# Attention's output kept transposed and undivided in DRAM, and divided in one last stage over four batches

## The chip, the cores and the metric

The kernel runs on one core of a Trainium2 chip. The metric is the device time of one execution in microseconds (us).

## The reference

The input `x` has 4 batches of 2048 tokens with 256 features. A first layer (a recurrence gated by a small expert network) and a second layer follow one another. The second layer, cut to what matters here:

```python
xn = _layernorm(x)
q, k, v = (xn @ W.T + b for each), reshaped to 16 heads of 16
a1 = softmax(q1 @ k1.T / 4); x1 = a1 @ v1     # heads 0 to 7
a2 = softmax(q2 @ k2.T / 4); x2 = a2 @ v2     # heads 8 to 15
s = concatenate([x1 - lv * x2, x2]) @ Wp.T + bp
g = silu(mixture_of_experts(xn))
return x + s * g
```

`lv` is one number worked out from four small vectors. Batches times heads make 64 attentions of 2048 queries by 2048 keys.

## The kernel before

The program runs in stages, each a block in which the five engines have instruction lists of their own and meet through semaphores. The first layer and the second layer's experts take the first 2640 us and are not touched. Then `attend` does the 64 heads, and `output_batch` does the projection and the last sum, once for each batch.

**`attend`.** A step is half a head: 1024 queries against all 2048 keys. There are 128 steps (`t`), two for each head (`half`), and each has eight slots (`sl`). In a slot TensorE's list is: three score products (`score`, keys by queries, 128x512), then the extra jobs of some slots, then two peak pairs (`peak`: the scores of the next step the other way round, 128 queries x 1024 keys), a fourth score product, and `values`: eight fp32 products of exponentials with values into O. O lies in bank 7 as 4 groups of 32 partitions by 256 queries; in each group 16 rows are features, and row 16 is the sum of the exponentials, since the values have a column of ones. ScalarE takes the exponential of each score tile (`at_E<-at_ps`), 32 a step. VectorE reduces every peak pair to its maxima (`at_mpart`), and at the end of a step these to `at_mx`.

Peak pairs and extra jobs use a ring of two pairs of banks: TensorE fills one when VectorE has freed it. There are two extra jobs. `turn` in slot 1 transposes `at_mx`; VectorE negates it (`at_mneg`), rounds it to bf16 (`at_mrow`), and takes the remainder as a second, low row; SP moves the two rows into `at_qs`, where the next step's scores subtract them. `normalise` in slot 3 brings the last step's O to queries by features: ScalarE's `copy_out` in slot 1 has put O into `at_osb`, TensorE transposes it in two products, VectorE inverts the eight sums of each query (`at_rec`) and multiplies into `at_A`, which holds all heads in SBUF. `values` of slot 1 starts the next O and waits for `copy_out`.

SP's list: sixteen loads for the head after the next, the values, and the rows of the two steps. GpSimd meanwhile joins the experts' results (`combine_experts`).

**`output_batch`.** For one batch: SP loads `f` (the experts' result) and `x1` (the residual), 2 MB each. VectorE combines the heads of `at_A` into `at_mix` (64 small operations over four batches for `x1 - lv * x2`, 64 copies), TensorE transposes them (32 products a batch), ScalarE copies them into `at_outT`, TensorE multiplies with `wp` (line 1586), VectorE adds the bias (line 1555) and multiplies with silu(f) (line 1558), GpSimd forms the silu and adds the residual (line 1570), and SP stores. A batch ends with a barrier.

## Time and profile before

| | |
|---|---|
| time, median of 3 runs | 5811.28 us (5802.47 to 5816.74) |
| the profiled execution | 5814.46 us, span 5813.0 us |
| granted TensorE clock, mean | 0.961 |
| busy share: TensorE, VectorE, ScalarE, GpSimd | 87%, 74%, 59%, 24% |

The span is from the first to the last instruction; the time of the execution is 1.5 us more. The profiled execution is 3.2 us slower than the median. Busy TensorE time is modelled, since its products are pipelined.

### The profile page before, as it was taken

The page shows a single profiled execution, that of the slowest core. Times are in us where ns is not written, and L with a number is a line of the kernel's source. Part 1 is how long each engine was busy: PE and PEld are TensorE (multiplying, and loading weights), DVE is VectorE, ACT ScalarE, POOL GpSimd, SP SyncE. Part 2 cuts the span into 40 slices and gives each one's busy share as a digit, 9 for nine tenths or more (in the row PEclk, how much of TensorE's full clock was granted, in tenths as well). Part 3 has the DMA queues.
Part 4 walks back from the last instruction along what each step waited for, and adds up shares of the span by engine and source line. Part 5 has one row for each costly group of instructions (what it writes and reads, how often), then busy time and mean ns, then how long its engine had stood idle before and what let it go on. Part 6 is the DMA issues. An engine that isn't in the chain of part 4 may idle for free. (4 is left out here: it accounts for less than half of the span.)

```text
span 5813.0 us, 94556 instructions
## 1 busy us (share of the span) xinstructions
PE 5028.4 (87%) x32123; PEld 2145.5 (37%) x32123; DVE 4317.1 (74%) x5419; ACT 3426.4 (59%) x5923; POOL 1419.5 (24%) x885
## 2 busy tenths in 40 slices
PE   5777777777767999996999999999999999999995
PEld 3233233233234566652333333333333333333334
DVE  5997987987971111115888888888888888888884
ACT  5765765666631111112767777777777777777772
POOL 1855846846850000004750000000000000000005
PEclk8998998998998999997999999999999999999998
DMA  3303003002022211213331111111111111111114
GB/s 100 106 15 116 0 28 104 1 30 87 1 78 83 72 61 62 65 61 86 101 87 32 34 30 29 29 29 34 32 29 29 29 32 34 29 29 29 29 39 163
DMA packets 351454, 299.33 MB, mean 51 GB/s; under 512 B 169184, under 2 KB 320992, under 8 KB 350432
## 3 DMA queue, kind: packets, MB, share of 16 engines
q1 hardware_dynamic: 336192, 251.90, 15.2%
q0 software_dynamic: 14848, 42.09, 2.4%
q8 instruction: 238, 3.90, 0.3%
q14 instruction: 176, 1.44, 0.1%
HBM read 175.78 MB, written 117.57 MB: 50 GB/s over the span
## 5 line engine op out<-in xcount | busy, mean ns | idle before, releaser
L1448 ACT ACTIVATE at_E<-at_ps 128x512 f32<-128x512 f32 x4096 | 2146.4, 604 | 836.3 <-PE at_ps L1356 821.3
L1465 DVE TENSOR_REDUCE at_mpart<-at_ps 128x1 f32<-128x1024 f32 x2080 | 2445.0, 1217 | 250.4 <-PE at_ps L1343 233.4
L1356 PE MATMUL at_ps<-at_qs,at_ks 98*128 98x512 bf16 x4096 | 1243.4, 385 | 19.7 <-ACT at_E L1448 17.1
L1364 PE MATMUL at_ps<-at_E,at_vst 128*32 128x256 f32 x16400 | 1101.7, 386 | 0.0
L1341 PE MATMUL at_ps<-at_ks,at_qs 64*128 64x512 bf16 x2080 | 697.1, 389 | 172.8 <-DVE at_A L1490 79.4
L1343 PE MATMUL at_ps<-at_kb,at_qb 64*128 64x512 bf16 x2080 | 697.2, 389 | 0.0
L1565 POOL TENSOR_TENSOR at_f<-at_f,at_sig 128x1024 f32<-128x1024 f32 x16 | 37.1, 2348 | 2696.3 <-ACT at_sig L1595 2696.3
L854 POOL TENSOR_TENSOR l_work<-l_work 128x1024 f32<-128x1024 f32 x256 | 604.5, 2361 | 78.7 <-DVE l_work L863 69.6
L1356 PEld LDWEIGHTS at_ps<-at_qs,at_ks 98*128 98x128 bf16 x4096 | 315.4, 97 | 832.3 <-ACT at_E L1448 572.4
L1364 PEld LDWEIGHTS at_ps<-at_E,at_vst 128*32 128x32 f32 x16400 | 428.7, 109 | 410.7 <-ACT at_E L1448 184.6
L750 PE MATMUL l_ps<-l_bc,l_sel 96*128 96x512 bf16 x1024 | 313.3, 395 | 289.3 <-DVE l_work L863 126.8
L1098 PE MATMUL ff_ps<-ff_xt,ff_w 128*128 128x512 f32 x1280 | 558.9, 595 | 0.8 <-ACT ff_xt L1144 0.8
L1151 ACT ACTIVATE ff_g<-ff_ps 128x512 f32<-128x512 f32 x160 | 95.5, 597 | 682.5 <-PE ff_ps L1098 682.4
L788 PE MATMUL l_ps<-l_work,l_ident 128*128 128x512 f32 x1024 | 483.6, 594 | 5.1 <-DVE l_work L884 5.1
L1166 DVE TENSOR_TENSOR ff_ht<-ff_g,ff_ps 128x512 f32<-128x512 f32 x160 | 110.1, 688 | 488.4 <-ACT ff_g L1151 488.4
L1341 PEld LDWEIGHTS at_ps<-at_ks,at_qs 64*128 64x128 bf16 x2080 | 182.8, 93 | 749.6 <-issue 331.2
L812 ACT ACTIVATE l_ps<-l_lnd,l_adec 128x1024 f32<-128x1024 f32 x256 | 286.0, 1117 | 241.1 <-DVE l_work L876 240.6
L848 POOL TENSOR_TENSOR l_work<-l_u,l_work 128x512 f32<-128x512 f32 x256 | 324.3, 1267 | 247.7 <-ACT l_work L799 247.7
L1098 PEld LDWEIGHTS ff_ps<-ff_xt,ff_w 128*128 128x128 f32 x1280 | 244.3, 191 | 291.8 <-issue 288.9
L884 DVE TENSOR_TENSOR l_work<-l_work,l_ps 128x1024 f32<-128x1024 f32 x256 | 312.1, 1219 | 0.3
L876 DVE TENSOR_TENSOR_SCAN l_work<-l_ps,l_carry,l_work 128x1024 f32<-128x1024 f32 x128 | 301.2, 2353 | 7.3 <-issue 7.3
L876 DVE TENSOR_TENSOR_SCAN l_work<-l_ps,l_work 128x1024 f32<-128x1024 f32 x128 | 292.4, 2284 | 16.5 <-ACT l_ps L812 10.3
(199 smaller groups left out, 4573.9 us busy)
## 6 DMA issues: line engine op xcount, KB each, us to landing
at_ks<-kp SPq DMA_DIRECT2D x396, 64.0 KB
ff_xin<-xd SPq DMA_DIRECT2D x41, 512.0 KB, 4.4
xd<-l_zero SPq DMA_DIRECT2D x4, 5120.0 KB, 33.2
yd<-ff_yout SPq DMA_DIRECT2D x40, 512.0 KB, 3.2
at_qs<-qp SPq DMA_DIRECT2D x132, 128.0 KB
at_qb<-qp SPq DMA_DIRECT2D x132, 128.0 KB
ff_w<-in_eW SPq DMA_DIRECT2D x9, 1024.0 KB, 5.8
at_kb<-kp SPq DMA_DIRECT2D x264, 32.0 KB
```

Source lines behind the costliest of these rows:

```text
L750: mm = pe.matmul(dst[:, q, :], m.sel[:, bass.ts(row, P)], m.bc3[:, t0 + BANK * q:t0 + BANK * (q + 1)], start=True, stop=True)
L788: mm = pe.matmul(y[:, q, :], m.ident[:], hc[i % 2][:, bass.ts(q, BANK)], start=False, stop=True, skip_group_check=True)
L848: pool.tensor_tensor(w[i % 2][:, HI], m.u[:, k, t0 + BANK:t0 + HALF], Bs[i % 2], ALU.mult).then_inc(s.wb, 1)
L854: pool.tensor_tensor(bx[i % 2], w[i % 2], inv[i % 2], ALU.mult).then_inc(s.bx, 1)
L876: dve.tensor_tensor_scan(h[i % 2], flat(pdec), bx[i % 2], m.carry[:, k, n:n + 1] if t0 else 0.0, ALU.mult, ALU.add).then_inc(s.h, 1)
L1098: mm = pe.matmul(HID[mt % 2][:, half, :], m.w1[:, e, k, col:col + P], m.xt[:, c % 2, k, :], start=(k == 0), stop=(k == KD - 1))
L1341: pe.matmul(ring[n % 2][:, 0, :], m.qs[0:64, buf, bass.ts(i, P)], m.ks[0:64, buf, bass.ts(2 * kh, BANK)], start=True, stop=True)
L1343: pe.matmul(ring[n % 2][:, 1, :], m.qb[64:P, buf, bass.ts(i, P)], m.kb[64:P, buf, bass.ts(kh, BANK)], start=True, stop=True).then_inc(s.ri ...
L1356: pe.matmul(S[chunk_bank(u, l)], m.ks[0:STACK + 2, j, bass.ts(kt, P)], m.qs[0:STACK + 2, j, half * QB + hf * BANK:half * QB + (hf + 1) * B ...
L1364: mm = pe.matmul(O[32 * q:32 * q + 32, :], m.vst[:, par, 2 * sl + kk, :], m.E[:, sl % 4, kk, bass.ts(q, QG)], start=(sl == 0 and kk == 0), ...
L1448: act.activation(m.E[:, sl % 4, c // 2, bass.ts(c % 2, BANK)], S[chunk_bank(u, l)], ACT.Exp, scale=SCALE).then_inc(s.ex, 1)
L1465: dve.tensor_reduce(m.mpart[:, job:job + 1], ring[n % 2].rearrange("p a b -> p (a b)"), AX_X, ALU.max).then_inc(s.ring_free, 1)
```

## The change

`at_A` and its division are gone from attention. `copy_out` puts O, as it stands, into one of two buffers, and SP stores its 4 x 17 rows (16 features and the sum, 256 queries each) into a DRAM tensor `ot` of heads x 17 x 2048. The extra job `turn` no longer uses the ring: its transpose goes to free columns of bank 7, behind the two peak pairs, and ScalarE negates and rounds, after the third exponential of slot 1; VectorE keeps the low row. `normalise` is gone. TensorE waits for `at_mneg` ahead of `values` in slot 1.

The last stage is one block for all four batches, in 16 jobs of 512 tokens. SP loads each batch's `ot` (features of all heads in the 128 partitions, tokens along the row), its sums (16 heads x 2048), `f` and `x1` into one of two buffers. VectorE inverts the 16x2048 sums in one instruction; TensorE spreads them over the 128 feature rows by a product with a selection matrix `hsel` of 16x128 (`spread`); VectorE multiplies and combines (`heads`); TensorE projects (`outputs`), without transposes; `finish` and GpSimd do the rest as before. In the diff, lines that only rename or allocate are left out.

```diff
-        s = stage_sems(nc, ctx, "att", "init loaded v_loaded v_free score ex av o_copy o2 ring ring_free mpart mfin mneg mhi mlo mrow rec")
+        s = stage_sems(nc, ctx, "att", "init loaded v_loaded v_free score ex av o_copy o_st0 o_st1 ring ring_free mfin turned mneg mhi mlo mrow")
         ring, S, O = [m.pair[0], m.pair[1]], [m.bank[4], m.bank[5], m.bank[6]], m.bank[7][:, 0:QG]
+        TURNED = m.bank[7][0:8, QG:QG + P]
...
-        NRING = 2 * SLOTS_A + 2
-        PRO = 4 * SLOTS_A + 1
-        EX0, AV0, RF0 = 3, 3, 2
+        NRING = 2 * SLOTS_A
+        PRO = 4 * SLOTS_A
+        EX0, AV0, RF0, OS0 = 3, 3, 2, 64
...
+                def store(t, slot, half, par):
+                    sp.wait_ge(s.o_copy, t + 1)
+                    for g in range(4):
+                        sp.dma_start(io.ot[bass.ds(slot, 1), :, half * QB + QG * g:half * QB + QG * (g + 1)].rearrange("o c t -> (o c) t"),
+                                     m.osb[32 * g:32 * g + HD + 1, par, :]).then_inc(o_st[par], 16)
...
+                        store(2 * h, h, 1, 0)
                         rows(2 * h + 2, 0, (j + 1) % 4)
+                        store(2 * h + 1, h + 1, 0, 1)
+                store(2 * HEADS, HEADS, 1, 0)
...
-                def turn(n, wait, mf):
+                def turn(mf):
                     pe.wait_ge(s.mfin, mf)
-                    pe.wait_ge(s.ring_free, wait)
-                    pe.transpose(ring[n % 2][0:8, 0, 0:P], m.mx[:], m.ident[:]).then_inc(s.ring, 1)
+                    pe.transpose(TURNED, m.mx[:], m.ident[:]).then_inc(s.turned, 1)
...
+                for q in range(4):
+                    pe.matmul(O[32 * q:32 * q + 32, :], m.vst[:, 1, q, :], m.E[:, 3, 0, bass.ts(q, QG)],
+                              start=True, stop=True, skip_group_check=True)
...
-                for q in range(4):
-                    pe.matmul(O[32 * q:32 * q + 32, :], m.vst[:, 1, q, :], m.E[:, 3, 0, bass.ts(q, QG)],
-                              start=True, stop=True, skip_group_check=True)
...
-                        if sl == TURN_AT:
-                            turn(PRO + local, w(), t + 2)
-                            local += 1
-                        if sl == NORM_AT:
-                            normalise(PRO + local, w(), t + 1)
-                            local += 1
                         for kh in range(2):
                             peak(8 * half + sl, kh, nxt, PRO + local, w())
                             local += 1
+                        if sl == TURN_AT:
+                            pe.wait_ge(s.o_copy, t + 1)
+                            turn(t + 2)
                         score(4 * sl + 3, u, t, j, half)
                         pe.wait_ge(s.ex, CHUNKS * t + 4 * sl + EX0)
-                        if sl == 1:
-                            pe.wait_ge(s.o_copy, t + 1)
+                        if sl == TURN_AT:
+                            pe.wait_ge(s.mneg, t + 2)
                         values((sl - 1) % SLOTS_A, (j if half or sl else j + 1) % 2)
```

ScalarE and VectorE in attention:

```diff
-                def copy_out(t):
+                act.sem_inc(o_st[0], OS0)
+                act.sem_inc(o_st[1], OS0)
+                def copy_out(t, par, stored):
                     act.wait_ge(s.av, SLOTS_A * t + 1 + AV0)
-                    act.wait_ge(s.o2, t + 1)
-                    act.copy(m.osb, O).then_inc(s.o_copy, 1)
-                def step(t, u):
+                    act.wait_ge(o_st[par], 64 * stored + OS0)
+                    act.copy(m.osb[:, par, :], O).then_inc(s.o_copy, 1)
+                def turn(t, first=False):
+                    act.wait_ge(s.turned, t + 2)
+                    if not first:
+                        act.wait_ge(s.mlo, t + 1)
+                    act.activation(m.mneg[:], TURNED, ACT.Identity, scale=-1.0).then_inc(s.mneg, 1)
+                    act.wait_ge(s.mneg, t + 2)
+                    if not first:
+                        act.wait_ge(s.mrow, 32 * (t + 1))
+                    act.copy(m.mrow[:, 0, :], m.mneg[:]).then_inc(s.mhi, 1)
+                def step(t, u, pairs):
                     for l in range(CHUNKS):
                         sl, c = l // 4, l % 4
+                        if sl == TURN_AT and c == 0:
+                            copy_out(t, u % 2, pairs)
                         act.wait_ge(s.score, CHUNKS * t + l + 1)
                         if c == 0:
                             act.wait_ge(s.av, SLOTS_A * t + sl - 2 + AV0)
                         act.activation(m.E[:, sl % 4, c // 2, bass.ts(c % 2, BANK)], S[chunk_bank(u, l)], ACT.Exp, scale=SCALE).then_inc(s.ex, 1)
-                        if sl == COPY_AT and c == 0:
-                            copy_out(t)
+                        if sl == TURN_AT and c == 2:
+                            turn(t)
+                turn(-1, first=True)
                 with act.Fori(0, HEADS // 4) as g:
                     for u in range(8):
-                        step(8 * g + u, u)
-                copy_out(2 * HEADS)
+                        step(8 * g + u, u, 4 * g + u // 2)
+                copy_out(2 * HEADS, 0, HEADS)
...
+                def low_row(t):
+                    dve.wait_ge(s.mhi, t + 2)
                     dve.tensor_tensor(m.mrow[:, 1, :], m.mneg[:], m.mrow[:, 0, :], ALU.subtract).then_inc(s.mlo, 1)
...
+                        if sl == TURN_AT:
+                            low_row(t)
```

The last stage (the function `output_batch` is removed whole); SP and TensorE, then VectorE, ScalarE and GpSimd:

```diff
+def output_batches(nc, io, m):
...
+        s = stage_sems(nc, ctx, "output", "o_in0 o_in1 f_in0 f_in1 rec spread heads1 heads0 mix out s_out sig silu prod sum st0 st1")
+        o_in, f_in, st = (s.o_in0, s.o_in1), (s.f_in0, s.f_in1), (s.st0, s.st1)
         PARTS = TILES // FT
+        JOBS = B * PARTS
+        R = [m.bank[0], m.bank[1], m.bank[2], m.bank[3]]
...
+                def load(b):
+                    p, h0 = b % 2, b * H1 + 1
+                    for k in range(KD):
+                        sp.dma_start(m.oT[:, p, k, :], io.ot[h0 + 8 * k:h0 + 8 * k + 8, 0:HD, :].rearrange("h c t -> h c t")).then_inc(o_in[p], 16)
+                    sp.dma_start(m.sums[:, p, :], io.ot[h0:h0 + H1, HD:HD + 1, :].rearrange("h o t -> (h o) t")).then_inc(o_in[p], 16)
+                    sp.dma_start(m.f[:, p, :, :], io.f[b:b + 1, :, :, :].rearrange("o p g (i d) -> (o p) (g i) d", d=D)).then_inc(f_in[p], 16)
+                    sp.dma_start(m.x1[:, p, :, :], io.x1[b:b + 1, :, :].rearrange("o (i p) d -> p (o i) d", p=P)).then_inc(f_in[p], 16)
...
+                load(0)
+                load(1)
+                for b in range(B):
+                    out = io.out[b:b + 1, :, :].rearrange("o (i p) d -> p (o i) d", p=P)
+                    for g in range(PARTS):
+                        sp.wait_ge(s.sum, PARTS * b + g + 1)
+                        sp.dma_start(out[:, bass.ts(g, FT), :], m.x1[:, b % 2, bass.ts(g, FT), :]).then_inc(st[b % 2], 16)
+                    if b + 2 < B:
+                        sp.wait_ge(st[b % 2], 16 * PARTS * (b // 2 + 1))
+                        load(b + 2)
+                for p in range(2):
+                    sp.wait_ge(st[p], 16 * PARTS * (B // 2))
...
+                def spread(j):
+                    b, g = j // PARTS, j % PARTS
+                    pe.wait_ge(s.rec, b + 1)
+                    if j >= 2:
+                        pe.wait_ge(s.heads0, j - 1)
+                    for k in range(KD):
+                        mm = pe.matmul(R[2 * (j % 2) + k], m.hsel[:, k, :], m.sums[:, b % 2, bass.ts(g, BANK)], start=True, stop=True)
+                    mm.then_inc(s.spread, 1)
+                def outputs(j):
+                    pe.wait_ge(s.mix, j + 1)
+                    for r in range(FT):
+                        n = FT * j + r
+                        if n >= 4:
+                            pe.wait_ge(s.s_out, n - 3)
+                        for c in range(KD):
+                            mm = pe.matmul(m.bank[4 + n % 4][:, 0:D], m.nT[:, j % 2, c, bass.ts(r, P)], m.wp[:, c, :],
+                                           start=(c == 0), stop=(c == KD - 1))
+                        mm.then_inc(s.out, 1)
+                spread(0)
+                for j in range(JOBS):
+                    if j + 1 < JOBS:
+                        spread(j + 1)
+                    outputs(j)
...
+                def heads(j):
+                    b, g = j // PARTS, j % PARTS
+                    p = b % 2
+                    if g == 0:
+                        dve.wait_ge(o_in[p], 48 * (b // 2 + 1))
+                        dve.reciprocal(m.sums[:, p, :], m.sums[:, p, :]).then_inc(s.rec, 1)
+                    dve.wait_ge(s.spread, j + 1)
+                    if j >= 2:
+                        dve.wait_ge(s.out, FT * (j - 1))
+                    dve.tensor_tensor(m.nT[:, j % 2, 1, :], m.oT[:, p, 1, bass.ts(g, BANK)], R[2 * (j % 2) + 1], ALU.mult).then_inc(s.heads1, 1)
+                    dve.tensor_tensor(m.n0[:, j % 2, :], m.oT[:, p, 0, bass.ts(g, BANK)], R[2 * (j % 2)], ALU.mult).then_inc(s.heads0, 1)
+                    dve.wait_ge(s.heads1, j + 1)
+                    dve.wait_ge(s.heads0, j + 1)
+                    dve.scalar_tensor_tensor(m.nT[:, j % 2, 0, :], m.nT[:, j % 2, 1, :], m.nlam[:, 0:1], m.n0[:, j % 2, :],
+                                             ALU.mult, ALU.add).then_inc(s.mix, 1)
+                def finish(j):
+                    b, g = j // PARTS, j % PARTS
+                    p = b % 2
+                    if j >= 2:
+                        dve.wait_ge(s.sum, j - 1)
+                    for r in range(FT):
+                        n = FT * j + r
+                        dve.wait_ge(s.out, n + 1)
+                        dve.tensor_tensor(m.s[:, j % 2, r, :], m.bank[4 + n % 4][:, 0:D], m.bp[:], ALU.add).then_inc(s.s_out, 1)
+                    dve.wait_ge(s.silu, j + 1)
+                    dve.wait_ge(s.s_out, FT * (j + 1))
+                    dve.tensor_tensor(m.s[:, j % 2, :, :], m.s[:, j % 2, :, :], m.f[:, p, bass.ts(g, FT), :], ALU.mult).then_inc(s.prod, 1)
+                for j in range(JOBS + 1):
+                    if j < JOBS:
+                        heads(j)
+                    if j:
+                        finish(j - 1)
...
+            @block.scalar
+            def _(act):
+                for j in range(JOBS):
+                    b, g = j // PARTS, j % PARTS
+                    act.wait_ge(f_in[b % 2], 32 * (b // 2 + 1))
+                    if j >= 2:
+                        act.wait_ge(s.silu, j - 1)
+                    act.activation(m.sig[:, j % 2, :, :], m.f[:, b % 2, bass.ts(g, FT), :], ACT.Sigmoid).then_inc(s.sig, 1)
...
+                def silu(j):
+                    b, g = j // PARTS, j % PARTS
+                    pool.wait_ge(s.sig, j + 1)
+                    pool.tensor_tensor(m.f[:, b % 2, bass.ts(g, FT), :], m.f[:, b % 2, bass.ts(g, FT), :], m.sig[:, j % 2, :, :], ALU.mult).then_inc(s.silu, 1)
+                silu(0)
+                silu(1)
+                for j in range(JOBS):
+                    b, g = j // PARTS, j % PARTS
+                    if j + 2 < JOBS and (j + 2) // PARTS == b:
+                        silu(j + 2)
+                    pool.wait_ge(s.prod, j + 1)
+                    pool.tensor_tensor(m.x1[:, b % 2, bass.ts(g, FT), :], m.x1[:, b % 2, bass.ts(g, FT), :], m.s[:, j % 2, :, :], ALU.add).then_inc(s.sum, 1)
+                    if j + 2 < JOBS and (j + 2) // PARTS != b:
+                        silu(j + 2)
```

How the instructions move. TensorE in slot 1 of the first step, before; `at_ident,at_mx` is the transpose of `turn`, `at_ks,at_qs` with `at_kb,at_qb` a peak pair, `at_qs,at_ks` a score, `at_E,at_vst` is `values`:

```order
L1356 MATMUL at_ps<-at_qs,at_ks 128x512 x3
L1350 MATMUL at_ps<-at_ident,at_mx 8x128
L1341 MATMUL at_ps<-at_ks,at_qs 128x512
L1343 MATMUL at_ps<-at_kb,at_qb 128x512
L1341 MATMUL at_ps<-at_ks,at_qs 128x512
L1343 MATMUL at_ps<-at_kb,at_qb 128x512
L1356 MATMUL at_ps<-at_qs,at_ks 128x512
L1364 MATMUL at_ps<-at_E,at_vst 32x256 x8
```

and after:

```order
L1369 MATMUL at_ps<-at_qs,at_ks 128x512 x3
L1355 MATMUL at_ps<-at_ks,at_qs 128x512
L1357 MATMUL at_ps<-at_kb,at_qb 128x512
L1355 MATMUL at_ps<-at_ks,at_qs 128x512
L1357 MATMUL at_ps<-at_kb,at_qb 128x512
L1363 MATMUL at_ps<-at_ident,at_mx 8x128
L1369 MATMUL at_ps<-at_qs,at_ks 128x512
L1377 MATMUL at_ps<-at_E,at_vst 32x256 x8
```

The transpose has moved behind the two peak pairs, and the fourth score and `values` follow it. In slot 3 the two products of `normalise` are gone, and it reads like any other slot.

ScalarE from the first exponential of slot 1, before; `at_osb` is `copy_out`:

```order
L1448 ACTIVATE at_E<-at_ps 128x512
L1437 REGISTER_ALU
L1438 REGISTER_ALU
L1439 COPY at_osb<-at_ps 128x256
L1444 REGISTER_ALU
L1448 ACTIVATE at_E<-at_ps 128x512
L1444 REGISTER_ALU
L1448 ACTIVATE at_E<-at_ps 128x512
L1444 REGISTER_ALU
L1448 ACTIVATE at_E<-at_ps 128x512
```

and after, from `copy_out`, which now stands ahead of that exponential:

```order
L1440 COPY at_osb<-at_ps 128x256
L1458 REGISTER_ALU
L1461 REGISTER_ALU
L1462 ACTIVATE at_E<-at_ps 128x512
L1458 REGISTER_ALU
L1462 ACTIVATE at_E<-at_ps 128x512
L1458 REGISTER_ALU
L1462 ACTIVATE at_E<-at_ps 128x512
L1444 REGISTER_ALU
L1446 REGISTER_ALU
L1447 ACTIVATE at_mneg<-at_ps 8x128
```

The negation stands behind the third exponential; one register instruction, the rounding (`at_mrow<-at_mneg`) and the fourth exponential follow it, and no table load stands anywhere in the loop. VectorE in the last stage, after, at the change from one batch to the next:

```order
L1595 SCALAR_TENSOR_TENSOR at_nT<-at_nT,at_nlam,at_n 128x512
L1606 TENSOR_TENSOR at_s<-at_ps,at_bp 128x256 x4
L1609 TENSOR_TENSOR at_s<-at_s,at_f 128x1024
L1587 RECIPROCAL at_sums<-at_sums 16x2048
L1591 TENSOR_TENSOR at_nT<-at_oT,at_ps 128x512
L1592 TENSOR_TENSOR at_n<-at_oT,at_ps 128x512
L1595 SCALAR_TENSOR_TENSOR at_nT<-at_nT,at_nlam,at_n 128x512
L1606 TENSOR_TENSOR at_s<-at_ps,at_bp 128x256 x4
```

The reciprocal of a batch stands ahead of that batch's `heads` and of the `finish` of the job before (lines 1606 and 1609 of the changed kernel).

## Rows read from the trace of the kernel before

**Rows 1.** Table by windows: stretch, its us, busy time (instructions), clock, DMA share, GB/s.

```profile
4000.00:4500.00 500.00, 477.80 (x4277) 167.16 (x4279) 439.60 (x483) 370.63 (x725) 0.00 (x0) 1.00 0.13 30
5662.00:5813.00 151.00, 86.86 (x384) 75.23 (x384) 73.25 (x208) 36.21 (x52) 74.68 (x32) 0.81 0.48 167
```

**Rows 2.** Timeline of VectorE, `at_A` of four steps: start us, us, engine, line.

```profile
2730.92 0.29 DVE L1490 TENSOR_TENSOR at_A<-at_ps,at_rec 128x128 f32 x1 [0.17 <-DVE at_rec L1488]
...
4094.59 0.29 DVE L1490 TENSOR_TENSOR at_A<-at_ps,at_rec 128x128 f32 x1 [0.16 <-DVE at_rec L1488]
...
4139.92 0.29 DVE L1490 TENSOR_TENSOR at_A<-at_ps,at_rec 128x128 f32 x1 [0.16 <-DVE at_rec L1488]
...
5661.41 0.29 DVE L1490 TENSOR_TENSOR at_A<-at_ps,at_rec 128x128 f32<-128x128 f32 x1
```

**Rows 3.** Timeline of TensorE, the `values` groups of one step.

```profile
4095.58 1.07 PE L1364 MATMUL at_ps<-at_E,at_vst 128*32 128x256 f32 x16
...
4098.19 1.07 PE L1364 MATMUL at_ps<-at_E,at_vst 128*32 128x256 f32 x16
...
4108.68 1.07 PE L1364 MATMUL at_ps<-at_E,at_vst 128*32 128x256 f32 x16
...
4111.87 1.07 PE L1364 MATMUL at_ps<-at_E,at_vst 128*32 128x256 f32 x16
...
4114.67 1.07 PE L1364 MATMUL at_ps<-at_E,at_vst 128*32 128x256 f32 x16
...
4118.30 1.07 PE L1364 MATMUL at_ps<-at_E,at_vst 128*32 128x256 f32 x16
```

**Rows 4.** Timeline, slot 3: the idle time before and its releaser in brackets.

```profile
4093.61 0.38 PE L1373 MATMUL at_ps<-at_ident,at_osb 128*128 128x128 f32 x2
...
4094.93 0.39 PE L1341 MATMUL at_ps<-at_ks,at_qs 64*128 64x512 bf16 x1 [0.62 <-DVE at_A L1490]
```

**Rows 5.** Timeline, slots 0 and 1 of the step of rows 3.

```profile
4107.58 2.06 ACT L1448 ACTIVATE at_E<-at_ps 128x512 f32<-128x512 f32 x4 [0.57 <-PE at_ps L1356]
...
4110.19 0.60 ACT L1448 ACTIVATE at_E<-at_ps 128x512 f32<-128x512 f32 x1 [0.55 <-PE at_ps L1356]
...
4110.35 0.27 PE L1350 MATMUL at_ps<-at_ident,at_mx 128*8 128x128 f32 x1
```

**Rows 6.** Groups by line and form: busy us, mean ns | idle before.

```profile
L1166 DVE TENSOR_TENSOR ff_ht<-ff_g,ff_ps 128x512 f32<-128x512 f32 x160 | 110.1, 688 | 488.4 <-ACT ff_g L1151 488.4
...
L1439 ACT COPY at_osb<-at_ps 128x256 f32<-128x256 f32 x129 | 47.4, 367 | 1.2 <-PE at_ps L1364 1.2
...
L1488 DVE RECIPROCAL at_rec<-at_ps 128x8 f32<-128x8 f32 x129 | 26.8, 208 | 75.0 <-PE at_ps L1373 75.0
...
L1555 DVE TENSOR_TENSOR at_s<-at_ps,at_bp 128x256 f32<-128x256 f32 x64 | 25.6, 419 | 47.6 <-PE at_ps L1586 47.5
...
L1558 DVE TENSOR_TENSOR at_s<-at_s,at_f 128x1024 f32<-128x1024 f32 x16 | 22.8, 1425 | 1.7
...
L302 DVE RECIPROCAL l_psmall<-l_psmall 128x16 f32<-128x16 f32 x4 | 1.0, 252 | 1.5 <-ACT l_psmall L536 1.5
...
L1664 ACT ACTIVATE at_lsum<-at_lsum 128x16 f32<-128x16 f32 x1 | 0.2, 216 | 8.7 <-DVE at_lsum L1651 8.7
...
L1651 DVE TENSOR_SCALAR at_lsum<-at_lsum 128x16 f32<-128x16 f32 x1 | 0.2, 174 | 0.0
```

**Rows 7.** The output stage: windows, timeline of GpSimd, DMA issues to landing.

```profile
5680.00:5690.00 10.00, 10.00 (x48) 8.82 (x47) 7.86 (x13) 0.00 (x0) 5.73 (x3) 1.00 0.15 52
...
5693.81 2.34 POOL L1570 TENSOR_TENSOR at_x<-at_x,at_s 128x1024 f32<-128x1024 f32 x1 [1.23 <-DVE at_s L1558]
...
at_f<-f SPq DMA_DIRECT2D x1, 2048.0 KB, 8.0
at_x<-x SPq DMA_DIRECT2D x1, 2048.0 KB, 13.4
out<-at_x SPq DMA_DIRECT2D x4, 512.0 KB, 2.9
```

141 lines of the change are left out of this document (24 added, 117 removed).

## The prediction

> **What bounds the kernel now.** The page's busy shares are averages over stages with different limits, so I read the two that the diff touches. The table by windows [rows 1] shows attention in steady state (4000 to 4500 us: TensorE busy 478 of 500 us, VectorE 440, ScalarE 371) and the output stage (5662 to 5813 us: nothing over 58%, clock 0.81). The timeline of `at_A` (one row a step, 129 in all) runs from 2730.92 to 5661.41 us [rows 2]: attention is 128 steps of 22.9 us, and whatever is saved in each counts 128 times. Two steps of the steady state (4094.59 to 4139.92) take 22.67 us each.
>
> Inside one step I read the starts of `values` [rows 3]. A plain slot takes 2.62 us (4095.58 to 4098.19 is one, 4098.19 to 4108.68 four of them), and TensorE issues without a hole in it. Slot 1 (turn) takes 3.19 us (to 4111.87), slot 2 takes 2.80 (to 4114.67), slot 3 (normalise) takes 3.63 (to 4118.30). The step is 22.72 us = 8 x 2.62 (20.96) + 0.57 + 0.18 + 1.01. So the two extra ring jobs cost 1.76 us in this step, and 22.67 - 20.96 = 1.71 in the mean of two; the rest is TensorE's.
>
> Why slot 3 costs 1.01: the two transposes enter the two-deep ring, VectorE first waits for them, then divides, and the second peak pair stands 0.62 us behind `at_A` [rows 4]. Slots 1 and 2 pay for the same thing through `at_mneg` and the late reduces.
>
> **The change part by part, attention.** (a) The normalise job leaves slot 3: two transposes, the reciprocal and the product go, and slot 3 becomes plain: -1.01 us. It frees VectorE of 0.50 us a step too, which waits for TensorE anyway in a plain slot.
>
> (b) Turn leaves the ring, and ScalarE negates and rounds. VectorE no longer delays the peaks, so slot 2 becomes plain: -0.18. VectorE keeps the low row (0.3 us), and has the slack of each slot to hide it in: idle 60 of 500 us [rows 1], 0.3 us of 2.62.
>
> (c) Slot 1 gets a new wait: `values` must wait for `mneg`, which ScalarE makes after the third exponential. Behind that wait stands all of TensorE's queue. In [rows 5] the first exponential of slot 1 starts at 4110.19. The copy of O now goes ahead of it; it can start when `values` of slot 0 ends (4108.68 + 1.07 = 4109.75, plus 0.06) and takes 0.37 us [rows 6], so it is done at 4110.18 and costs nothing. Three exponentials at 0.52 us each (four took 2.06 us, [rows 5]) end their issue at 4111.75. The transpose is ready by then: in the old place it began at 4110.35, and it now goes behind two peak pairs, about 4111.3, + 0.27. The negation is a small activation: between 0.22 us (128x16) and 0.37 us (copy of 256 columns) [rows 6]; I take 0.29 for 128 columns. `values` can then start at about 4111.75 + 0.29 + 0.08 = 4112.12, that is 3.44 us after the last: an excess of 0.82 in place of 0.57. The rounding copy (0.29) and the fourth exponential follow while TensorE does `values` (1.0 us), and the next scores come after that. Excess after: 0.82 + 0 + 0; before 1.71 in the mean. Saved: 0.88 us a step, 128 x 0.88 = **113 us**. Bounds: if ScalarE pays for the copy and each own wait in full (0.37 + 0.1), 0.4 a step; if the negation hides wholly, 1.15 us.
>
> (d) SP's queue gets four stores a step (17 rows of 1 KB each). Queued behind a store's wait are the next rows of maxima and, after the second, the next load; each of these is issued half a step and more ahead of use. I cost them at nothing; without that cover each would be four issues of some 0.5 us. Only the last one shows: copy, four issues and the landing (2.9 us for an `out` store, [rows 7]) in place of transposes, reciprocal and product: **+4 us**. The prologue's accumulation start now precedes the first peaks, and VectorE waits there once for ScalarE: **+1 us**. The order of ScalarE shows no table load in the loop, so none is in the sum.
>
> **The output stage.** Today it is four batches one after the other, each with load, work, store and barrier: the first one's last sum ends at 5693.81 + 2.34 = 5696.15 [rows 7], and only its stores are left before the next load; 151 us in all [rows 1]. The new one overlaps loads and stores, and its floor is an engine:
>
> - TensorE, a quarter batch (job): eight 256-column matmuls and two of 512. At full clock 48 records of 256 columns took 10.0 us [rows 7], two records a matmul, so 0.42 us each: 3.4 + 1.7 = 5.1 us.
> - VectorE, a job: two products and one combination of 512 columns at 0.69, four additions at 0.42, one product of 1024 at 1.43 [rows 6]: 5.2 us. The two alternate, some 5.3 us a job.
> - VectorE also inverts the sums, 16 partitions x 2048 elements in one instruction, where before they lay 8 on each of 128 lanes. A lane still does one after the other. No row has this size. The 16-element reciprocal takes 252 ns and a plain operation of 16 elements 174 [rows 6]: 78/16 = 4.9 ns an element over the plain 1.04, so about 6 ns; 8 elements in 208 ns give the same. 2048 x 6 = 12.3 us; I take **12.5 us**. Bounds: 2.3 us (at the plain rate, 1.1 ns an element), and 53 us (208/8 = 26 ns, nothing of the small one being fixed). I take a value near the low end, since a plain operation of 16 elements shows that 0.15 us and more of the small one is fixed.
>
> The Trainium skill speaks against this edit: "VectorE: DVE Perf Modes", section "First, the fixed hardware budget", says that the reciprocal runs as an iterated divide with a repeat count of 8. At eight of its 0.96 GHz cycles an element, 2048 would take an estimated 17 us, 4.6 us a batch more than my value. The same slope on 16 elements would leave 0.12 us of the 252 ns as fixed, less than any row here leaves.
>
> Nothing covers the reciprocal: `spread(4b)` waits for it, `heads(4b)` for that, and it stands ahead of `finish` of the job before, so TensorE runs dry and its first spread comes cold (1.7 us at 2.4 GHz, 3.4 at 1.2; I take 3). A batch: 12.5 + 3 + 4 x 5.3 = 36.7 us; four, 147. Ahead of it the first `ot` load (2 MB and the sums: 8.0 us as for `at_f` [rows 7], up to 13.4 if it shares the engines as `at_x` does; I take 9), behind it the last sum and store (2.35 + 2.9 + issue, 7). Together 163 us against 151: **+12 us**. All later loads (6 MB, some 20 us where 4 MB took 13.4) have 30 us and more.
>
> **The sum.** The profiled execution is 5814.5 us, 3.2 over the median of the runs: 5814.5 - 113 + 1 + 4 + 12 = 5718.5, as a median **5715 us**.
>
> **The rivals.**
> 1. *The reciprocal is dearer, some 16 us*: only half of the 252 ns is fixed, so 126/16 = 7.9 ns an element. For it: a slope out of 8 and 16 elements is carried to 2048. Then 4 x 3.6 = +14 us: 5729 us. The page of the Trainium skill named above would make it 17 us each and 5733.
> 2. *The reciprocal costs no more than a plain operation*, 2.3 us. Then the jobs alone bound the stage: 16 x 5.5 + 9 + 3 + 12 = 112 us, and the kernel takes 5664 us. Against it: 252 against 174 ns.
> 3. *The wait for `mneg` takes back half of the saving.* ScalarE pays for the copy, since it can't start the first exponential at once, and its own two waits; `values` starts 0.5 us later: 128 x 0.5 = +64, 5779 us. For it: ScalarE is idle only 0.55 us ahead of a slot's first exponential [rows 5], and now has 0.95 us of extra work in one.
> 4. *Slower than before:* the reciprocal goes as the whole small row, 26 ns an element, 53 us. Then the stage gets 4 x 40.5 = 162 us longer: 5877 us. It decides from 36 us an instruction (12.5 + 96/4), 18 ns an element. Against it: 1 to 16 elements of other operations cost 153 to 174 ns, so most of the 208 is fixed.
>
> **How the numbers follow.** A measurement of this kernel tells 0.3% (17 us) from no change. Chances: forecast 0.60 (own range 5695 to 5730), rival 1 0.18, rival 2 0.07, rival 3 0.10, rival 4 0.03, and 0.02 for something that gives no change. The range 5682 to 5762 leaves out rivals 2 and 4 and the worse half of 3. All but rival 4 and the last lie more than 17 us under 5811: faster 0.95.
>
> **What the changed profile would show.** Steps of 21.8 us between two copies of O; `values` intervals of 2.62 in slots 2 and 3 and 3.4 in slot 1, with TensorE waiting there for `at_mneg`; `at_mneg` on ScalarE near 0.29 us; four reciprocals of 16x2048 near 12.5 us; an output stage of about 163 us whose chain is VectorE's. I am wrong if slot 1 grows to 4 us, if slot 2 pays for ScalarE's lateness, if the stores delay rows or loads so that steps start late, or if loads of `ot` come later than 13 us or hold up a batch.

## The result, and the profile after

The changed kernel takes 5778.5 us (median of 5 runs, 5771.0 to 5779.2), the kernel before in the same measurement 5811.0: a ratio of 0.9942 [0.9929, 0.9954], 33 us faster. I had forecast 5715 us with a range up to 5762. The profiled execution has a span of 5776.7 us and a mean clock of 0.953.

Attention did what was forecast. TensorE's `values` in one step, on its timeline (start us, us; in brackets the idle time before and its releaser), to be held against [rows 3]:

```profile
4089.87 1.07 PE L1377 MATMUL at_ps<-at_E,at_vst 128*32 128x256 f32 x16
...
4093.23 1.07 PE L1377 MATMUL at_ps<-at_E,at_vst 128*32 128x256 f32 x16 [0.31 <-ACT at_mneg L1447]
...
4095.84 1.07 PE L1377 MATMUL at_ps<-at_E,at_vst 128*32 128x256 f32 x16
...
4098.47 1.07 PE L1377 MATMUL at_ps<-at_E,at_vst 128*32 128x256 f32 x16
...
4111.57 1.07 PE L1377 MATMUL at_ps<-at_E,at_vst 128*32 128x256 f32 x16
```

Slot 1 takes 3.36 us and ends in the new wait for `at_mneg`; slots 2 and 3 take 2.61 and 2.63. Two copies of O stand 21.61 us apart (timeline of ScalarE), and the last of the 129 starts at 5534.31, where the last row of `at_A` started at 5661.41 in [rows 2]:

```profile
4091.10 0.37 ACT L1440 COPY at_osb<-at_ps 128x256 f32<-128x256 f32 x1 [0.27 <-PE at_ps L1377]
...
4112.71 0.37 ACT L1440 COPY at_osb<-at_ps 128x256 f32<-128x256 f32 x1 [0.18 <-PE at_ps L1377]
...
5534.31 0.37 ACT L1440 COPY at_osb<-at_ps 128x256 f32<-128x256 f32 x1 [1.19 <-PE at_ps L1377]
```

The output stage did not. Its table by windows (us, busy time by engine, clock, DMA share, which is the busy share of the 16 DMA engines, GB/s), where [rows 1] has 151 us for the old one:

```profile
5536.00:5778.00 242.00, 106.77 (x320) 66.83 (x320) 141.09 (x132) 17.75 (x17) 85.33 (x32) 0.68 0.64 141
5540.00:5545.00 5.00, 0.00 (x0) 0.00 (x0) 0.00 (x0) 1.28 (x1) 0.00 (x0) 0.50 0.55 115
5545.00:5550.00 5.00, 0.00 (x0) 0.00 (x0) 0.00 (x0) 0.00 (x0) 0.00 (x0) 0.50 1.05 161
5550.00:5555.00 5.00, 0.00 (x0) 0.00 (x0) 0.00 (x0) 0.00 (x0) 0.00 (x0) 0.50 0.95 154
```

No compute engine works between 5545 and 5555, and the DMA engines are full at about 155 GB/s. VectorE's four reciprocals say who waits:

```profile
5568.95 12.94 DVE L1587 RECIPROCAL at_sums<-at_sums 16x2048 f32<-16x2048 f32 x1 [34.66 <-DMA at_sums<-ot]
5607.77 12.93 DVE L1587 RECIPROCAL at_sums<-at_sums 16x2048 f32<-16x2048 f32 x1
5665.29 12.94 DVE L1587 RECIPROCAL at_sums<-at_sums 16x2048 f32<-16x2048 f32 x1 [14.49 <-DMA at_sums<-ot]
5723.97 12.94 DVE L1587 RECIPROCAL at_sums<-at_sums 16x2048 f32<-16x2048 f32 x1 [15.42 <-DMA at_sums<-ot]
```

The first batch, once its load had landed, took 38.8 us to the next reciprocal (5568.95 to 5607.77; forecast 36.7), the next two 57.5 and 58.7, of which 14.5 and 15.4 are waits for a load. The chain that ended last (start us, us, what) passes three times through the same load, 27, 26 and 27 us from issue to landing:

```profile
5541.65 27.27 DMA at_sums<-ot
5568.95 12.95 DVE at_sums L1587
...
5639.16 26.10 DMA at_sums<-ot
...
5696.87 27.08 DMA at_sums<-ot
```

The chain names the sums because they are issued last under one semaphore with the features. I had forecast 9 us for the first load; this is three times as much.

### The profile page after: what moved, and what is told of

It is laid out like the page before. It is cut to its first block and busy times, and to the rows that moved or that the text cites. A ratio compares the mean times of both kernels' runs of the same rounds, so it can differ in the third digit from the quotient of the medians.

```text
span 5776.7 us, 94576 instructions
## 1 busy us (share of the span) xinstructions
PE 4975.4 (86%) x31801; PEld 2097.1 (36%) x31801; DVE 4269.3 (74%) x4827; ACT 3454.1 (60%) x6146; POOL 1431.3 (25%) x885
## 5 line engine op out<-in xcount | busy, mean ns | idle before, releaser
L1355 PE MATMUL at_ps<-at_ks,at_qs 64*128 64x512 bf16 x2080 | 656.0, 388 | 24.4 <-DVE at_mpart L1479 20.5
L1357 PE MATMUL at_ps<-at_kb,at_qb 64*128 64x512 bf16 x2080 | 656.0, 388 | 0.0
```

What stands on the lines that cost most here:

```text
L1355: pe.matmul(ring[n % 2][:, 0, :], m.qs[0:64, buf, bass.ts(i, P)], m.ks[0:64, buf, bass.ts(2 * kh, BANK)], start=True, stop=True)
L1357: pe.matmul(ring[n % 2][:, 1, :], m.qb[64:P, buf, bass.ts(i, P)], m.kb[64:P, buf, bass.ts(kh, BANK)], start=True, stop=True).then_inc(s.ri ...
```

## The experiments

The kernel before ran beside each group: 5807.5 us beside e1 to e4, 5808.1 beside e5 to e8, 5812.6 beside e9 to e12. Ratios are to it.

### Which transfer is late, and why

**e1_by_head** loads each head's 16 rows with a DMA of its own.

```diff
-for k in range(KD):
-    sp.dma_start(m.oT[:, p, k, :], io.ot[h0 + 8 * k:h0 + 8 * k + 8, 0:HD, :]...)
+for n in range(H1):
+    sp.dma_start(m.oT[HD * (n % 8):HD * (n % 8) + HD, p, n // 8, :], io.ot[h0 + n:h0 + n + 1, 0:HD, :]...)
```

> The changed kernel, with one edit: the last stage loads a batch's 16 heads of ot by 16 DMAs of 16 rows of 8 KB each in place of two DMAs of 8 heads x 16 rows. Same rows, same bytes, same places. In the changed kernel the first sums (issued right behind the two loads) landed 27.3 us after their issue, and those of the third and fourth batch 26.1 and 27.1. Theory A (a DMA whose outermost dimension on the DRAM side is 8 runs on only half of the 16 engines, and everything issued behind it on these waits for it): the sums land about 9 us after the loads are issued, VectorE's waits of 34.7, 14.5 and 15.4 us ahead of the reciprocals become some 20, 0 and 0, and the kernel takes 5778 - 45 = about 5733 us. Theory B (the rows of ot are slow to read, by their address or since they are long, whatever engine reads them): no change, 5778 us. Theory C (the loads behind it, f, x1 and the next batch's, share the rate): no change either. The issue of 14 more DMAs, some 7 us of SP, costs up to 4 us of the gain.

Measured 5746.5 us, 0.9883 [0.9865, 0.9901], 13 us more than theory A had. The waits before the reciprocals fell to 24.5, 0, 5.6 and 6.4 us. The DMA engines were all busy, but slow, 139 to 149 GB/s in three windows of the load; two of them:

```profile
5542.00:5547.00 5.00, 0.00 (x0) 0.00 (x0) 0.00 (x0) 0.00 (x0) 0.00 (x0) 0.50 1.05 139
5547.00:5552.00 5.00, 0.00 (x0) 0.00 (x0) 0.00 (x0) 0.00 (x0) 0.00 (x0) 0.50 1.08 143
```

So the form of the load (into how many pieces it falls, and over which partitions) costs at least 30 us, and the new form isn't right yet.

**e2_sums_first** loads the sums first, on a semaphore of their own, and the reciprocal waits for these alone.

> The changed kernel, with one edit: the sums are loaded ahead of ot's two loads on a semaphore of their own, and the reciprocal waits for the sums alone; the heads job waits for ot. By all theories of the slow load the reciprocal (12.9 us) then runs while ot's loads are on their way, where the load is what is waited for: first, third and fourth batch. Expected: the first reciprocal starts about 3 us after the issue (before: 28.7 after the first load's issue), 3 x 12.9 = 39 us saved, 5740 us, while ot itself still lands 26 us and more after its issue. If the load's length was only apparent (sums last in a queue, ot long landed), the heads jobs start right after the reciprocal and the saving is 25 us a batch, some 70 us in all.

Measured 5747.2 us, 0.9889 [0.9871, 0.9907]. No reciprocal after the first waits for a DMA: its 13 us now run beside the load of `ot`. In the first batch the products wait 12.4 us more for `ot` itself, so the features, and not only the sums, were late. That treats the symptom, and is worth 31 us (39 expected).

**e3_ot_alone** lets SP wait until the first batch's `ot` and sums have landed before it issues anything else.

> The changed kernel, with one edit: of the first batch, ot's two loads and the sums are issued alone, and SP waits until they have landed before it issues f, x1 and the second batch. It measures the load by itself. Theory A (half of the engines): DMA share near 0.5 and the load about as long as before, 2.1 MB in 20 us or more. Theory B (rows slow to read on any engine): share near 1.0, as long as before. Theory C (the rate is shared with f, x1 and the next batch): it lands in 8 to 10 us, as f did in the kernel before. One look; the total says little, since f and x1 come later.

Measured 5765.2 us in one run. SP issues at 5532.21 and gets on at 5553.34: 21 us for 2.1 MB with nothing beside it:

```profile
5532.21 1.39 SPq L1534 DMA_DIRECT2D at_oT<-ot  x2
5533.65 0.45 SPq L1535 DMA_DIRECT2D at_sums<-ot  x1
5553.34 0.36 SPq L1538 DMA_DIRECT2D at_f<-f  x1
```

Windows of that time, and one when `f` and `x1` move:

```profile
5540.00:5545.00 5.00, 0.00 (x0) 0.00 (x0) 0.00 (x0) 0.00 (x0) 0.00 (x0) 0.50 0.51 118
5545.00:5550.00 5.00, 0.00 (x0) 0.00 (x0) 0.00 (x0) 0.00 (x0) 0.00 (x0) 0.50 0.49 120
5555.00:5560.00 5.00, 0.00 (x0) 0.00 (x0) 5.00 (x1) 0.00 (x0) 0.00 (x0) 0.50 0.90 373
```

A share of 0.5 could be sixteen engines busy half of the time. The packets in the trace say that it is eight: between 5540 and 5550 eight of them are under way in 87% of the time and nine in 12%, while in the windows of e4_split and e9_gap_sixteen below it is sixteen and more. Each of the eight engines moves 15 GB/s where the later window has 26 (373 / 16 / 0.9).

**e4_split** keeps features and sums in two DRAM tensors, so that a load is 128 rows without a gap between heads.

```diff
-scratch("ot", (HEADS + 1, HD + 1, L), F32)
+scratch("ot", (HEADS + 1, HD, L), F32); scratch("os", (HEADS + 1, L), F32)
...
-io.ot[h0 + 8 * k:h0 + 8 * k + 8, 0:HD, :].rearrange("h c t -> h c t")
+io.ot[h0 + 8 * k:h0 + 8 * k + 8, :, :].rearrange("h c t -> (h c) t")
```

> The changed kernel with ot split in two DRAM tensors: features (heads x 16 x 2048) and sums (heads x 2048). A store is then 4 DMAs of 16 rows and 4 of one row in place of 4 of 17, and a load of 8 heads is one run of 128 rows of 8 KB without a gap (outermost dimension 128 on both sides). Theory A: as by head, the sums land within 9 to 10 us, 5778 - 45 = 5733 us, and without the 14 extra issues. Theory B in the form of the gap after each head's 16 rows: the same; in the form of the length of the rows: no change. If storing 17 rows in one DMA was slow as well (17 doesn't divide by anything), the stores land sooner: the 5.5 us between the last copy of O and the first load of the last stage shrink to 4. SP issues four more DMAs a step, which should be hidden.

Measured 5725.5 us, 0.9848 [0.9831, 0.9865]: 53 us less than the changed kernel. The four stores more in each step cost nothing: from the first copy of O to the last it is 2807.5 us, and 2807.6 in the changed kernel. The load runs at 382 GB/s and nothing waits for one after the first:

```profile
5545.00:5550.00 5.00, 0.00 (x0) 0.00 (x0) 0.00 (x0) 0.00 (x0) 0.00 (x0) 0.50 0.96 382
```
```profile
5552.73 12.94 DVE L1589 RECIPROCAL at_sums<-at_sums 16x2048 f32<-16x2048 f32 x1 [14.16 <-DMA at_sums<-os]
5592.03 12.93 DVE L1589 RECIPROCAL at_sums<-at_sums 16x2048 f32<-16x2048 f32 x1
5635.20 12.93 DVE L1589 RECIPROCAL at_sums<-at_sums 16x2048 f32<-16x2048 f32 x1
5677.28 12.93 DVE L1589 RECIPROCAL at_sums<-at_sums 16x2048 f32<-16x2048 f32 x1
```

**e7_eight_by_sixteen** is e4_split with the load written as 8 by 16 rows again.

> As e4_split (sums in a tensor of their own, 16-row stores, no gap between heads), but the loads of ot keep the form of 8 heads by 16 rows that the changed kernel has. Theory A (the number 8 of the outermost dimension puts a load on half the engines): the first batch's ot lands after 20 us or more as in the changed kernel, and the time goes back to 5755 to 5780 us. Rival B (the gap of one row after each 16 is what slows it, or the form makes no difference when the rows are contiguous): as e4_split, landing about 8 us, 5725 us.

Measured 5723.5 us, 0.9855 [0.9838, 0.9872], as e4_split. Theory A had 5755 us or more. Without a gap the 8 by 16 rows are one run of 128 equal steps, and this run can't tell whether they were joined on the way to the DMA. Rival B (the gaps) stood, so the next run was made to separate gaps from the number of pieces.

**e9_gap_sixteen** has gaps, but 16 pieces: an unused row lies after features 0 to 7 of each head.

```diff
+scratch("ot", (HEADS + 1, HD + 2, L), F32)
...
+io.ot[h0 + 8 * k:h0 + 8 * k + 8, :, :].rearrange("h (a c) t -> (h a) c t", a=2)[:, 0:8, :]
```

> The changed kernel with 18 rows a head in ot: features 0 to 7, a row that nothing uses, features 8 to 15, the sums. A load of 8 heads is then 16 pieces of 8 rows with a gap behind each piece (the changed kernel: 8 pieces of 16 rows with a gap; e4_split: 128 rows without a gap). Theory A (the number of pieces, 8 against 16, is what leaves half of the engines out): ot lands in about 8 us and the time is that of e4_split, 5715 to 5735 us. Rival B (the gaps slow a load, whatever the number of pieces): landing 20 us or more, 5760 us or more.

Measured 5735.4 us, 0.9865 [0.9848, 0.9881]; one load lands after 11.7 us.

```profile
5540.00:5545.00 5.00, 0.00 (x0) 0.00 (x0) 0.00 (x0) 0.00 (x0) 0.00 (x0) 0.50 1.03 244
5545.00:5550.00 5.00, 0.00 (x0) 0.00 (x0) 0.00 (x0) 0.00 (x0) 0.00 (x0) 0.50 1.07 220
```

All engines work now (share 1.03), at 13 to 15 GB/s each, about as in e3_ot_alone. So there are two factors: eight pieces occupy half of the engines, and each engine is slower than in e4_split. A packet of 8 KB takes 0.58 us in the windows of e3_ot_alone, 0.60 here and 0.31 in e4_split (medians). For the first factor, the Trainium skill ("DMA: Bandwidth & Descriptors", section "Why a DMA increments its semaphore by 16 and not by 1") says that the slowest dimension on each side of a transfer sets how many engines it uses, by the largest number up to 16 that divides both: 8 pieces into 128 partitions give 8 engines, 16 pieces give 16. The 0.49 to 0.51 of e3_ot_alone and the 1.03 here agree with it.

The time is between the two theories and nearer to A: 43 of the 53 us of e4_split come with this edit. But it changes two things at once, since a piece now writes 8 neighbouring partitions and not 16, and e1_by_head tells how little the first one does alone: there sixteen engines were busy, each load on 16 neighbouring partitions, and moved 139 to 149 GB/s against the 118 to 120 of eight engines, as a packet of 8 KB took 0.96 us. No run has eight engines on partitions that lie apart, so how the 43 us divide between the two is not shown.

**e13_head_no_gap** and **e14_pitch_32** ask for the second factor: e4_split's tensor with e1_by_head's loads, and the changed kernel with 32 rows a head instead of 17. They ran on a chip on which the kernel before took 6001.6 us, so they are read by ratios and windows. (The pitch is the distance from one head to the next.)

> e4_split (no gaps, 128 rows a load, 23 GB/s an engine), but with the loads of ot cut by head, 16 of 16 rows a batch, as in e1_by_head. In e1_by_head all engines were busy and still moved only 136 to 156 GB/s together. Theory A (the gap after each 16 rows had no part in that, since each of its loads was contiguous; what slows an engine is that all 16 write to the same 16 partitions at a time): 130 to 160 GB/s here too and 5740 us or more. Rival B (the layout with the row between slows every row's read): 350 GB/s or more, 5730 us or less.

> The changed kernel with 32 rows a head in ot instead of 17: still 8 pieces of 16 rows a load, with gaps of 16 rows. Theory A (8 pieces use half of the engines, whatever the pitch, each writing 16 neighbouring partitions): as the changed kernel, 5770 to 5785 us, windows of its first load at 150 to 180 GB/s. Rival B (the odd pitch of 17 rows of 8 KB is the trouble): loads as in e4_split, 5725 to 5740 us.

Measured: e13_head_no_gap 5935.2 us (median of three runs; a fourth took 13591.6 us and isn't used), 0.9897 [0.9877, 0.9917], the ratio of e1_by_head; e14_pitch_32 5960.8 us, 0.9938 [0.9917, 0.9960], that of the changed kernel. So loads by head are as slow without a gap, and the odd pitch isn't what slows the 8 pieces; neither is needed for the second factor. That the gaps have no part in the 10 us between e9_gap_sixteen and e4_split was not tried. One window of e13_head_no_gap and one of e14_pitch_32 (the windows beside it have 187 and 143 GB/s):

```profile
5730.00:5735.00 5.00, 0.00 (x0) 0.00 (x0) 0.00 (x0) 0.00 (x0) 0.00 (x0) 0.50 1.01 148
```
```profile
5727.00:5732.00 5.00, 0.00 (x0) 0.00 (x0) 0.00 (x0) 0.00 (x0) 0.00 (x0) 0.50 0.97 159
```

**e15_step_eight** (the kernel before 5999.9 us) changes only which SBUF partitions a load of e13_head_no_gap writes. The rows of `wp` don't follow, so its output isn't the kernel's, but the work is the same.

```diff
-sp.dma_start(m.oT[HD * (n % 8):HD * (n % 8) + HD, p, n // 8, :], ...)
+sp.dma_start(m.oT[n % 8:P:8, p, n // 8, :], ...)
```

> As e13_head_no_gap (16 loads of 16 rows a batch), but the 16 rows of head n go to the partitions n, n + 8, n + 16 ... in place of 16 neighbours; the selection matrix follows, the rows of wp don't, so the projection multiplies features by the weights of others (the same work). The Trainium skill, page SBUF — State Buffer, section Door 1: The DMA port swizzle, says that four neighbouring partitions, and those 32 above them, share one of 16 ports. Theory A (that is what slowed e13: 16 rows on 4 ports): 8 ports are reached, the first windows of the load go from 148 to over 200 GB/s, VectorE's wait before the first reciprocal falls from 22.1 us to 16 or 17, the later waits of 5 us vanish, and the ratio falls from 0.990 to about 0.986. Rival B (many small loads are slow for another reason, as the work per load): windows stay at 140 to 155 GB/s and the ratio at 0.989 to 0.990.

Measured 5927.6 us, 0.9874 [0.9858, 0.9891]; the intervals overlap, so the time alone shows nothing, but the trace decides. A load lands 2.8 us after its issue instead of 8.1, with 205 and 234 GB/s while the engines aren't even full, since SP's issues (0.63 us for each 128 KB) set the pace; the first wait is 18.5 us instead of 22.1, the last two 0.5 and 0.8 instead of 5.8 and 5.3:

```profile
5735.00:5740.00 5.00, 0.00 (x0) 0.00 (x0) 0.00 (x0) 0.00 (x0) 0.00 (x0) 0.50 0.68 205
5740.00:5745.00 5.00, 0.00 (x0) 0.00 (x0) 0.03 (x1) 0.00 (x0) 0.00 (x0) 0.50 0.85 234
```

The second factor in the loads by head is therefore the write side: sixteen engines on sixteen neighbouring partitions get in each other's way. That the same holds of the changed kernel's 8 pieces, each engine on 16 neighbours of its own, fits its 118 to 120 GB/s if the engines go through them in step, but neither this nor the step was tried by itself.

### The other terms

**e5_lanes** lays the sums over 128 lanes.

```diff
-sb("hsel", [H1, KD, P]); sb("sums", [H1, 2, L])
+sb("hsel", [P, 8, KD, P]); sb("sums", [P, 2, L // 8])
```

> As e4_split, but the sums of a batch lie over 128 lanes of 256 elements (16 heads by 8 chunks of positions) instead of 16 lanes of 2048, and the selection matrices are one pair for each chunk. Theory A (the 12.94 us of a reciprocal stand whole on VectorE's path, once a batch, and follow the elements of a lane): each falls to about 256 x 6.3 ns = 1.6 us, so 4 x 11.3 = 45 us go, and some 3 come back for 1 MB more of constants: 5725.5 - 42 = 5684 us. Rival B (VectorE isn't what the stage waits for between batches; TensorE, GpSimd or a load takes the place): less than half of it comes, 5705 us or more.

Measured 5679.0 us, 0.9776 [0.9759, 0.9792]: 46.5 us less than e4_split, theory A. A reciprocal of 128x256 takes 1.74 us, and four that are shorter by 12.94 - 1.74 us make 44.8 us.

**e6_turn_early** moves `turn` between the two peak pairs.

```diff
-                        if sl == TURN_AT:
-                            pe.wait_ge(s.o_copy, t + 1)
-                            turn(t + 2)
+                            if sl == TURN_AT and kh == 0:
+                                pe.wait_ge(s.o_copy, t + 1)
+                                turn(t + 2)
...
-if sl == TURN_AT and c == 2:
+if sl == TURN_AT and c == 1:
```

> As e4_split, but in slot 1 of attention TensorE's transpose of the maxima stands between the two peak pairs and ScalarE's two operations on it come one exponential earlier (after the second, not the third). Theory A (the 0.74 us that slot 1 is longer than the others is the wait for mneg, whose chain starts at the transpose): the chain starts about 0.5 us earlier, slot 1 falls from 3.36 us to some 2.85, a step from 21.6 to 21.1, and 129 steps give 60 us: 5665 us (5650 to 5685). Rival B (the exponentials are then late instead, or the transpose waits for the copy of O): the step stays at 21.6 us and the time at 5725 us within 10.

Measured 5674.5 us, 0.9764 [0.9747, 0.9781]: 51 us less than e4_split. Slot 1 takes 2.93 us and shows no wait for `at_mneg`; its second row here is the transpose of `turn`:

```profile
4087.41 1.07 PE L1379 MATMUL at_ps<-at_E,at_vst 128*32 128x256 f32 x16
...
4089.49 0.27 PE L1365 MATMUL at_ps<-at_ident,at_mx 128*8 128x128 f32 x1
...
4090.34 1.07 PE L1379 MATMUL at_ps<-at_E,at_vst 128*32 128x256 f32 x16
...
4092.95 1.07 PE L1379 MATMUL at_ps<-at_E,at_vst 128*32 128x256 f32 x16
```

The 0.3 us that slot 1 is still longer than the next slot (2.61) is this transpose: the second peak pair starts 0.53 us behind the first, and in the next slot 0.22.

**e8_no_silu** and **e11_no_pool** leave GpSimd's work out, the silu product in one, that and the last sum in the other.

> As e4_split, but GpSimd's product f * sigmoid(f) is left out of the output stage (the output is then computed with f in place of silu(f)). Theory A (VectorE's 128x512 operations take 1.27 us in the mean instead of 0.75 because GpSimd works on SBUF at the same time): the products and the scalar_tensor_tensor fall to 0.9 us or less, a job from 6.05 to 5.4 us, 16 jobs give 10 us: 5715 us. Rival B (they are slow for another reason, as PSUM operands or the loads): their means stay, 5725 us.

> As e4_split, but GpSimd's two operations of a job are left out of the output stage, the product f * sigmoid(f) and the addition to x (what is stored is x without the addition). Theory A (VectorE's operations that read and write SBUF alone slow down while GpSimd works): the scalar_tensor_tensor falls from a mean of 1.27 us to 0.75 and the product from 1.67 to 1.23, so a job of VectorE from 6.05 to about 4.9 us unless TensorE (5.1) takes over: 16 x 1 us and some 3 us of tail give 5705 us. Rival B (slow for another reason): the means stay and only the tail goes, 5722 us.

Measured 5722.7 us, 0.9853 [0.9836, 0.9870], and 5720.8 us, 0.9838 [0.9822, 0.9854]: nothing that can be told from e4_split. The slowdown is there all the same. Groups of VectorE in e4_split, then in e11_no_pool (last columns: busy us, mean ns):

```profile
L1611 DVE TENSOR_TENSOR at_s<-at_s,at_f 128x1024 f32<-128x1024 f32 x16 | 26.8, 1674 | 1.7
...
L1597 DVE SCALAR_TENSOR_TENSOR at_nT<-at_nT,at_nlam,at_n 128x512 f32<-128x512 f32 x16 | 20.4, 1273 | 1.7
```
```profile
L1611 DVE TENSOR_TENSOR at_s<-at_s,at_f 128x1024 f32<-128x1024 f32 x16 | 19.6, 1225 | 1.7
L1597 DVE SCALAR_TENSOR_TENSOR at_nT<-at_nT,at_nlam,at_n 128x512 f32<-128x512 f32 x16 | 12.0, 751 | 1.7
```

Without GpSimd the two fall by 0.45 and 0.52 us; in e8_no_silu only the product does (1.24 us; the combination stays at 1.29 beside GpSimd's sum). A job falls from 6.05 to 5.56 us and not to 4.9, because VectorE now waits 0.16 and 0.44 us for TensorE in each. My expectation had given both gains to the time, but TensorE took half of them. From one reciprocal to the next it is 39.0, 40.4 and 40.7 us in e11_no_pool and 39.3, 43.2 and 42.1 in e4_split: 4 us over three batches. The medians of the times lie 5 us apart, and their intervals overlap.

**e10_lanes_turn** is e5_lanes and e6_turn_early together; **e12_invert_ahead** also puts the next batch's reciprocal one job earlier.

```diff
+invert(0)
 for j in range(JOBS + 1):
     if j < JOBS:
         heads(j)
+        if j % PARTS == PARTS - 1 and j + 1 < JOBS:
+            invert(j // PARTS + 1)
```

> e4_split with the edits of e5_lanes and e6_turn_early together. They lie in different stages, so their gains should add: 5725.5 - 46.5 - 51 = 5628 us (5620 to 5640). A rival would be that a shared wait hides one of them: 5650 us or more.

> As e10_lanes_turn, but the reciprocal of the next batch stands one job earlier on VectorE, before the last job's four additions, so that TensorE's spread of the next batch doesn't wait for it at the turn of a batch. In e5_lanes VectorE waited 3.9 us there for the spread, at three turns, and the additions of the last job came late: 3 x 4 to 5 us, 5628 - 13 = 5615 us. Rival (TensorE now waits for the reciprocal at the same place, in front of the last job's outputs): 5625 us or more.

Measured 5628.1 us, 0.9675 [0.9659, 0.9691], and 5615.5 us, 0.9662 [0.9646, 0.9679]. The gains add: 5725.5 - 46.5 - 51 = 5628; that it fits to the microsecond is luck, since each interval is some 9 us to either side. The step from the first to the second, 12.6 us by the medians, is not clear of noise by the two intervals, which overlap; the trace has 79.4 us from the first reciprocal to the last in place of 90.2. e12_invert_ahead is the best version: 197 us less than before in its comparison (5812.6), 163 less than the changed kernel.

## Why the prediction was wrong

The time was 63.5 us above the forecast, all of it in the output stage.

- **Step 22.67 to 21.8 us (a, b, c).** Right in the mechanism, a little low in size. Most steps are 21.6 to 21.8 us (21.93 in the mean, 22.94 before), slots 2 and 3 are plain. The excess of slot 1 is 0.74 (0.82 forecast), `at_mneg` takes 250 ns (0.29), and the copy costs nothing. From the first copy of O to the last it is 2807.6 us, and 2935.8 in the kernel before (2724.36 to 5660.16 on its timeline): 128 saved, or 127 by the two ends (5661.41 and 5534.31), where 113 were forecast. Rival 3 did not come: it needs an excess of 1.3 us in slot 1, and that its 5779 us is nearly the measured time is chance. What slot 1's excess is made of, e6_turn_early showed: the wait for `mneg` was 0.43 of the 0.74 us, and taking it away gave 51 us; the rest is the transpose.
- **Stores hidden, +4 and +1 (d).** Right within 2 us: the last copy starts at 5534.31, and the first load is issued at 5540.22, 5.9 us later.
- **Reciprocal 12.5 us.** Right, 12.94, and it lies bare on the path, as e5_lanes showed. That is 6.3 ns an element; the slope from [rows 6] gave 6. The estimate of 17 us from the Trainium skill's repeat count ("VectorE: DVE Perf Modes", "First, the fixed hardware budget") is not what this size takes. Rivals 1, 2 and 4 fall.
- **Spread and jobs, 3 + 4 x 5.3.** Too low. The cold spread takes 3.8 us and a steady job 6.05: the combination of 512 columns takes 1.27 us in the mean, not 0.69, and the product 1.67, not 1.43, beside GpSimd. The batch without a late load took 38.8 in place of 36.7, and others of e4_split 42 to 43. With 0.44 a reciprocal, 0.8 a spread and 0.75 a job, that makes some 17 us over four batches.
- **The step that failed: "I take 9" for the first load of `ot`, and "all later loads (6 MB, some 20 us ...) have 30 us and more".** I priced 2 MB of `ot` by the rate of `at_f` in [rows 7], which is a transfer of another form: 128 rows, one a partition, in equal steps. `ot` came as 8 pieces of 16 rows on 16 neighbouring partitions each. It takes 21 us alone (e3_ot_alone) and 27 beside the other loads, which are late too (`at_f` lands after 27.6 us, the median of four, in place of 8.0). VectorE stood 34.7 us before the first batch, of which some 13 were forecast, and 14.5 and 15.4 us before the last two. That is 21 + 30 = 51 us of the stage's excess; e4_split, which changes the form of the load and leaves attention as long as it was, gave 53 us back and came to within 11 us of the forecast.

The profiled execution lies 60 us above the 5718.5 of the sum: 51 for the load, 17 for spread and jobs, some 5 for a longer tail, less the 15 that attention saved beyond the forecast, are 58. So the load is the miss, and the other errors cancel in part, which is luck. The last 3.5 us of the 63.5 are the 3.2 that the sum took off for the median: this time the profiled execution is the median. I did name late loads of `ot` among what would make me wrong, but gave them no rival, no price and no chance.

## What to carry to other kernels

A transfer is priced by its form, not by its bytes: look for a row with the same outermost count and the same spread over partitions, and where there is none, price it by the slowest form that a row shows. A layout in DRAM that saves a store (17 rows in one go) can cost more in the load; equal rows over 128 partitions, in one piece, were worth 53 us here. To keep more engines busy is not enough where they write the same few partitions (e1_by_head). An instruction on few lanes that nothing covers adds its whole length to every batch (e5_lanes, 46 us), and a wait that comes once a step is worth the small move that takes it away (e6_turn_early, 51 us).

## What the runs showed of the hardware

- 2.1 MB in 8 pieces of 16 rows: DMA share 0.5, eight packets under way and 118 to 120 GB/s (e3_ot_alone). In 16 pieces of 8 rows: all engines, 220 to 244 (e9_gap_sixteen). As 128 rows: 382 (e4_split).
- Loads of 16 rows of 8 KB: 148 GB/s and 8.1 us each on 16 neighbouring partitions (e13_head_no_gap), 234 GB/s and 2.8 us on every eighth partition (e15_step_eight). The Trainium skill ("SBUF — State Buffer", "Door 1: The DMA port swizzle") has 4 ports for the first and 8 for the second; the runs agree in direction. In size they are above it: for partitions 0 to 15 that page has 104 GB/s, and the loads by head moved 139 to 151.
- VectorE's `scalar_tensor_tensor` of 128x512 takes 0.75 us without GpSimd's work (e11_no_pool) and 1.27 in the mean beside it (e4_split); its products with one operand in PSUM (0.68) did not change.
- SP's issue of the second batch's first load in the changed kernel lasted 30.6 us, with five transfers issued before it. That looks like a full queue; everything behind it on SP waits. What fills it was not tried.
